# A transformer block with attention and routed experts, one core: the closing drain of POOL's descriptor generator is left out, and ACT computes the roots of the last four tiles instead of three

## The reference

```python
# attention: weights W + A @ B, batch norm over q, k, v, causal softmax, two projections
x = _layernorm(x + _L0_attn_ref(x, ...), axis=-1)

# experts
logits = _ln(xf, router_ln_scale, router_ln_bias) @ router_w.T + router_b
probs = softmax(logits); topw, topi = top_k(probs, 2); topw = topw / sum(topw)
def expert(ls, lb, W1, B1, W2, B2):
    h = gelu(_ln(xf, ls, lb) @ W1.T + B1)
    return h @ W2.T + B2
out = einsum('te,etd->td', gates, [expert(...) for each e])
x = _layernorm(x + out, axis=-1)

def _layernorm(x, axis=-1, eps=1e-05):
    return (x - mean(x)) / sqrt(var(x) + eps)
```

## Time and profile before

| | us |
|---|---|
| median of 3 runs | 425.51 (423.96 to 427.02) |
| the profiled execution, its time | 424.67 |
| the profiled execution, its span | 422.9 |
| PE busy in it | 403.4 (95%) |
| DVE, ACT, POOL busy | 281.1, 323.8, 321.0 |

### The profile page before, as it was taken

The page is one execution under the profiler, slowest core; times in us unless marked ns, Lnnn a source line. Parts: engine busy times, 40 slices in busy tenths (PEclk is TensorE's granted clock), DMA queues, the critical chain, the costliest instruction groups (busy, mean ns, idle before and its releaser), DMA issues.

```text
span 422.9 us, 14560 instructions
## 1 busy us (share of the span) xinstructions
PE 403.4 (95%) x3446; PEld 387.8 (92%) x3446; DVE 281.1 (66%) x1674; ACT 323.8 (77%) x830; POOL 321.0 (76%) x606
## 2 busy tenths in 40 slices
PE   8999999999997999999999999999999999999980
PEld 7968899998896999999999999999999999999980
DVE  2444899999999667556565555446766667666662
ACT  1228799999897688777887887888788888888851
POOL 7000189888889888888888787748888888788885
PEclk9999999999998999999999999999999999999996
DMA  9999611111115523545544555643333343423211
GB/s 228 316 403 390 136 48 44 47 47 48 42 55 150 110 61 91 134 139 138 148 118 124 134 146 150 162 118 90 109 96 105 112 107 105 109 84 108 65 33 37
DMA packets 45490, 51.69 MB, mean 122 GB/s; under 512 B 6610, under 2 KB 37074, under 8 KB 45410
## 3 DMA queue, kind: packets, MB, share of 16 engines
q1 hardware_dynamic: 37312, 31.46, 28.1%
q0 software_dynamic: 7728, 18.51, 13.0%
q10 hardware_dynamic: 370, 0.80, 0.6%
HBM read 28.23 MB, written 21.72 MB: 118 GB/s over the span
## 4 chain that ended last, share of the span: by engine, by line
PE 47%; POOL 27%; issue 11%; DVE 6%; SPq 4%; DMA 3%; ACT 1%; POOLq 1%; DVEq 0%
PE bank L877 17%; PE bank L892 17%; POOL queue L583 11%; POOL idle L567 5%; POOL r_z L611 5%; POOL out L617 4%; PE bank L694 3%; PE bank L867 2%; PE bank L685 2%; DMA x_all<-x 1%; SPq L442 1%; POOL queue L604 1%; DVE x_all L1266 1%; SPq L435 1%; SPq L444 1%
## 5 line engine op out<-in xcount | busy, mean ns | idle before, releaser
L877 PE MATMUL bank<-xT 128*128 128x128 f32 x1136 | 152.0, 277 | 0.0
L892 PE MATMUL bank<-w2T,xT 128*128 x1136 | 150.3, 275 | 0.4 <-DVE yt L1440 0.4
L892 PEld LDWEIGHTS bank<-w2T,xT 128*128 128x128 f32 x1136 | 138.3, 192 | 0.6 <-issue 0.6
L877 PEld LDWEIGHTS bank<-xT 128*128 128x128 f32 x1136 | 138.7, 193 | 0.0
L929 ACT ACTIVATE xT<-w1T,zero_col 128x512 f32 x139 | 100.4, 722 | 41.7 <-issue 36.6
L1440 DVE TENSOR_TENSOR yt<-bank,b_bc 128x128 f32<-128x128 f32 x142 | 41.5, 292 | 88.4 <-PE bank L892 78.4
L617 POOL DMA_INDIRECT out<-xT,xg x71 | 75.8, 1067 | 16.8 <-issue 16.5
L604 POOL DMA_INDIRECT queue<-xT,xg x71 | 72.1, 1016 | 17.6 <-POOL idle L602 13.7
L1070 ACT ACTIVATE xT<-bank 128x512 f32<-128x512 f32 x142 | 82.1, 578 | 2.2 <-PE bank L877 2.2
L583 POOL DMA_INDIRECT queue<-x_all x64 | 62.2, 972 | 11.5 <-issue 6.7
L929 ACT ACTIVATE xT<-bank,one_col 128x128 f32<-128x128 f32 x142 | 52.1, 367 | 11.5 <-PE bank L867 5.6
(11 more groups left out here) (227 smaller groups left out, 727.2 us busy)
## 6 DMA issues: line engine op xcount, KB each, us to landing
xg<-queue SPq DMA_DIRECT2D x71, 129.5 KB, 2.2
xg<-queue SPq DMA_DIRECT2D x71, 67.5 KB, 2.4
x_all<-x SPq DMA_DIRECT2D x16, 256.0 KB, 6.1
xT<-x_t SPq DMA_DIRECT2D x8, 512.0 KB, 9.9
w1r<-w_t SPq DMA_DIRECT2D x8, 256.0 KB, 5.9
w2T<-w_t SPq DMA_DIRECT2D x8, 256.0 KB, 11.5
queue<-xT,xg POOLq DMA_INDIRECT x71, 2.7
out<-xT,xg POOLq DMA_INDIRECT x71, 2.4
```

Of the source, the lines that this page charges most:

```text
L877: last = mm(bank[2 + s][:, h * P:(h + 1) * P], w1c[:, (q - 1) % WR, h * P:(h + 1) * P], xgT[:, s, :], start=True, stop=True)
L892: last = mm(bank[4 + s][:, 0:P], hs[:, s, h, :], w2T[:, bass.ds(e, 1), h, :].rearrange("p a d -> p (a d)"), start=(h == 0), stop=(h == HC ...
```

## The change

Two things are changed. The block is opened with `no_gpsimd_drain=True`, and BY_ACT goes from 3 to 4.

```diff
-        BY_SP, BY_ACT = 3, 3
+        BY_SP, BY_ACT = 3, 4
...
-        block = ctx.enter_context(nc.Block())
+        block = ctx.enter_context(nc.Block(no_gpsimd_drain=True))
```

## The result

The changed kernel takes 423.28 us (median of 20 runs, 421.74 to 425.46) and the kernel before 425.43 us (median of 20 runs): a ratio of 0.9955, with a 95% interval of 0.9941 to 0.9969. That is 1.9 us by the ratio and 2.15 us by the medians. 423.1 was forecast. The profiled execution took 423.76 us with a span of 422.0 us, so 1.76 us lie around it (1.77 before).

The account below looks back on a forecast made before the run. The prediction took POOL's back-to-back scatters, then POOL's drain past SP's arrival, to bound the kernel's tail. Root 0.56 us plus drain 1.8 us made 2.4 us, so 425.5 − 2.4 = 423.1 us, range 421.8 to 424.4.

Parts of the forecast that it names:

- The drain: Closing barrier: without POOL's drain, SP waits some 0.3 us instead of 2.1; gain 1.8 us, bounds 1.6 and 2.1.
- the hop to POOL: Closing barrier: SP's signal must reach POOL before the release; taken as 0.1 us, between nothing and 0.24.
- The root: POOL's tail: moving tile 138's root to ACT starts the last scatter 0.56 us earlier; bounds 0.42 and 0.84.
- The rival of a tail bound by DVE: Kernel's tail: DVE, not POOL, is the bound, so the moved root gives 0.25 us; time 423.5 us; chance 0.04.
- The count on POOL's side: POOL's last scatters: without the root between, the pitch falls from 1.96 to 1.40 us, a gain of 0.56 us.
- ACT's cover: ACT, tile 138: the root is ready at 411.91, 0.73 us before DVE can use it, so ACT's side costs nothing.
- The end of the drain waited for outside the barrier: After the barrier: the program still waits for the generator's closing work; gain only 0.56 us, median 424.9 us; chance 0.22.
- Slower, because the work starts later and in full: Behind the barrier: the closing work's 3.46 us start at 420.5, not 419.20; median 426.6 us; chance 0.08.
- The sum: Whole kernel: 0.56 + 1.8 = 2.4 us saved, so the median falls from 425.5 to 423.1 us.

Follow-up runs that it names:

- DVE reordered: Changed kernel with DVE's step for tile 141 reordered: finish of 139, moments and variance of 140, then sum of 141; ratio 0.9926, again 0.9938, to the kernel before.
- five roots: Changed kernel with BY_ACT = 5 instead of 4, so one root more moves from POOL to ACT; ratio 0.9953 to the kernel before.

## Why the prediction was right

- **The drain.** 1.8 us with bounds of 1.6 and 2.1 were forecast; 1.9 us were measured, in the changed kernel and with the flag alone. SP was the last to arrive. Its wait at the barrier fell to 0.2 us where 0.3 was taken, since the hop to POOL, put at 0.1 us, is shorter than that: in the trace SP's signal starts at 421.821 and POOL's answer at 421.863.
- **The root.** 0.56 us with bounds of 0.42 and 0.84 were forecast; 0.15 us were measured, outside the bounds. The step that failed is "so POOL stays the bound by 0.3 to 0.8 us, and DVE's pace doesn't enter". It compared the end of DVE's instruction with the start of the scatter as if one could follow the other at once. Wherever a scatter waited for DVE, it started 0.81 us behind DVE's end. With that, in the kernel before, tile 139 was ready for its scatter at 414.84 + 0.81 = 415.65, and the scatter came at 415.71.

So that scatter could move up by 0.06 us of its own, and not by 0.56; the 0.31 us of margin that the forecast left it was 0.50 too little to hold the 0.81. The rest had to come from DVE. Its `finish` of tile 139 came 0.18 us earlier against PE (415.50 − 411.42 against 414.52 − 410.26) and took 0.07 us longer, which gives 0.11. Together that is 0.17 us, and the scatter of tile 139 moved up by just that (5.45 to 5.28 us behind PE's last group); 0.02 of it is gone again in the pitch of 1.30 behind it.

The rival of a tail bound by DVE, put at 0.04, was right about what holds the scatter of tile 139, and its 0.25 us for DVE's head start was nearer. DVE's `finish` of tile 138 did start 0.34 us earlier, but 0.19 of it was lost before `add_bias` of tile 141, where DVE idled 0.53 us (above) and before the change 0.34:

```profile
413.64 0.29 DVE L1440 TENSOR_TENSOR yt<-bank,b_bc 128x128 f32<-128x128 f32 x1 [0.34 <-issue]
```

What lengthened that gap no row shows. The count on POOL's side was sound: with DVE reordered the moved root gave 0.64 us, inside the bounds of 0.42 and 0.84.

- **ACT's cover.** This held: the logarithm started 0.04 us behind its variance, and the root was ready at 413.06, 0.65 us before DVE used it (0.7 forecast).
- **The end of the drain waited for outside the barrier.** No: the time around the span stayed at 1.7 to 1.8 us in the runs of the changed kernel.
- **Slower, because the work starts later and in full.** Its mechanism is real, since a late drain does cost its full 3.5 us; but nothing behind this barrier asks for one. The drain put back behind the landing shows what such a request would have cost: slower than before.
- **The sum.** 2.4 us were forecast, and the rows give 2.05: 0.1 more for the drain and 0.4 less for the root. That 423.1 came so near 423.28 is owed to the drain, which is nine tenths of the gain; the mechanism given for the root was wrong, and its miss is too small to show in the time. The gain forecast and the gain measured both lie far under the 4.3 us named as what a single measurement tells, but the comparison of 20 runs with 20 is finer.

## What to carry to other kernels

Look at who arrives last at the closing barrier and what it was doing. If it is POOL's drain, and another engine already waits for every scatter to land, the drain's part past that engine's arrival was plain gain here, and it is read from one row. When work is taken off a back-to-back engine, the margin of its next input must be counted to where the engine can start on it, with the latency that the trace shows between such a pair, and not to where the input was finished. Then ask which step of the feeding engine can be put first; here that gave 0.5 us on top of the 0.15 of the moved root. The new order without the moved root wasn't run.

## What the runs showed of the hardware that I had not expected

- A drain on POOL costs 3.5 us when many scatters came before it, even when it starts 1.3 us after the last one ended and with its data landed. A second one behind it costs 0.034 us, and the opening one, with no scatter before it, 0.17 us. Behind the first 2 scatters it ended 1.6 us after them, behind 34 more 2.9 us.
- From the end of the DVE instruction that a scatter waits for to the start of that scatter it is 0.81 us, in the changed kernel, with the root alone, with five roots and in the reordered kernel alike. A scatter whose data are long there starts 0.30 us behind the end of the scatter before it.
